# A fused attention and mixture-of-experts layer on one core: coefficient rows by DMA from HBM in place of a selector matmul, and three PSUM banks each for gate and up

## What is computed

```
scores = sigmoid(x @ router_w.T);  topk_idx, topk_w = route(x)      # 8 of 64 experts, from 4 of 8 groups
coef = zeros((T, E)).at[arange(T)[:, None], topk_idx].add(topk_w)
g = einsum('th,ehi->tei', x, Wg);  u = einsum('th,ehi->tei', x, Wu)
h = silu(g) * u * coef[:, :, None]
moe_out = einsum('tei,eih->th', h, Wd)
shared = silu(x @ SWg) * (x @ SWu) @ SWd
x + moe_out + shared
```

## Time and profile before

| what | value |
|---|---|
| median of 3 runs (lowest to highest) | 1395.52 us (1395.37 to 1397.26) |
| time of the profiled execution | 1397.18 us |
| its span, first to last instruction | 1395.5 us |
| PE, busy share of the span | 97% |
| POOL | 81% |
| DVE | 77% |
| ACT | 63% |
| mean granted TensorE clock | 0.990 |

### The profile page before, as it was taken

The page is one execution under the profiler, slowest core; times in us unless marked ns, Lnnn a source line. Parts: engine busy times, 40 slices in busy tenths (PEclk is TensorE's granted clock), DMA queues, the critical chain, the costliest instruction groups (busy, mean ns, idle before and its releaser), DMA issues.

```text
span 1395.5 us, 37217 instructions
## 1 busy us (share of the span) xinstructions
PE 1347.2 (97%) x12985; PEld 776.2 (56%) x12985; DVE 1075.9 (77%) x1906; ACT 875.9 (63%) x1588; POOL 1130.1 (81%) x2235
## 2 busy tenths in 40 slices
PE   3999999999999999999988999999999999999998
PEld 1566666666666666666656544444444444444443
DVE  6788888877888877888878778687777777786765
ACT  4677766666666666666666565656565655656554
POOL 2888888888888888888988887878786877878776
PEclk8899999999999999999999999999999999999999
DMA  7233333333333333333321000000000000000000
GB/s 188 72 81 76 81 76 81 75 83 78 84 75 83 83 83 78 79 77 79 89 58 47 9 1 8 9 9 8 4 15 0 16 1 16 1 16 0 1 8 8
DMA packets 84851, 67.60 MB, mean 48 GB/s; under 512 B 27793, under 2 KB 75217, under 8 KB 84689
## 3 DMA queue, kind: packets, MB, share of 16 engines
q1 hardware_dynamic: 84688, 65.52, 18.9%
HBM read 13.05 MB, written 2.10 MB: 11 GB/s over the span
## 4 chain that ended last, share of the span: by engine, by line
PE 77%; DVE 8%; issue 5%; POOL 5%; ACT 3%; SPq 1%; DMA 1%; DVEq 0%; ACTq 0%; POOLq 0%
PE bank L1048 74%; POOL arena L532 3%; DVE arena L1006 3%; PE bank L1234 2%; POOL arena L494 1%; DVE arena L1012 1%; ACT arena L690 1%; DVE arena L951 1%; DMA arena<-in_L_attn_bk 0%; ACT arena L650 0%; ACT arena L654 0%; DVE arena L901 0%; PE bank L1258 0%; ACT arena L671 0%; DVE arena L971 0%
## 5 line engine op out<-in xcount | busy, mean ns | idle before, releaser
L1048 PE MATMUL bank<-arena 128*128 128x512 f16 (+4 forms) x12600 | 1318.4, 265 | 33.0 <-DVE arena L982 7.3
L1048 PEld LDWEIGHTS bank<-arena 128*128 128x128 f16 (+2 forms) x12600 | 731.9, 98 | 586.2 <-DVE arena L1012 21.0
L494 POOL TENSOR_TENSOR arena<-arena 128x256 f16<-128x256 f32 x1024 | 597.2, 615 | 101.4 <-ACT arena L650 100.5
L532 POOL TENSOR_TENSOR arena<-arena 128x128 f16<-128x128 f32 x1056 | 423.1, 436 | 118.3 <-ACT arena L695 114.6
L951 DVE TENSOR_REDUCE arena<-bank 128x2 f32<-128x1024 f32 x256 | 312.1, 1220 | 53.8 <-PE bank L1048 49.7
L650 ACT ACTIVATE arena<-bank 128x512 f32<-128x512 f32 x512 | 276.8, 595 | 63.2 <-PE bank L1048 63.2
L695 ACT ACTIVATE arena<-arena 128x512 f16<-128x512 f32 x264 | 165.7, 628 | 158.6 <-DVE arena L1012 157.0
L1006 DVE TENSOR_TENSOR arena<-arena,bank 128x512 f32<-128x512 f32 x256 | 175.2, 684 | 108.1 <-ACT arena L690 79.9
L1012 DVE TENSOR_TENSOR arena<-arena,bank 128x512 f32<-128x512 f32 x256 | 176.1, 688 | 29.3 <-DVE arena L1006 4.5
L690 ACT ACTIVATE arena<-bank 128x512 f32<-128x512 f32 x264 | 154.9, 587 | 56.8 <-PE bank L1048 54.0
L639 ACT ACTIVATE arena<-bank,arena 128x512 f16<-128x512 f32 x128 | 88.0, 687 | 143.0 <-PE bank L1048 143.0
(11 more groups left out here) (107 smaller groups left out, 426.3 us busy)
## 6 DMA issues: line engine op xcount, KB each, us to landing
arena<-arena SPq DMA_DIRECT2D x384, 128.0 KB, 2.4
arena<-in_L_attn_x SPq DMA_DIRECT2D x9, 256.0 KB, 2.9
arena<-in_L_ffn_Wg SPq DMA_DIRECT2D x32, 64.0 KB, 2.2
arena<-in_L_ffn_Wu SPq DMA_DIRECT2D x32, 64.0 KB, 2.2
arena<-in_L_ffn_Wd SPq DMA_DIRECT2D x32, 64.0 KB, 2.1
out<-arena SPq DMA_DIRECT2D x8, 256.0 KB, 2.3
arena<-in_L_attn_Wq SPq DMA_DIRECT2D x1, 512.0 KB, 3.9
arena<-in_L_attn_Wk SPq DMA_DIRECT2D x1, 512.0 KB, 5.0
```

The lines of the kernel that those rows point to most:

```text
L494: last = pool.tensor_tensor(num_lo[:, u % 2, s, h, q], num[:, u % 2, s, h, q], num_hi[:, u % 2, s, h, q, 1], ALU.subtract)
L532: last = pool.tensor_tensor(hid_lo[:, r, at], hid[:, r, at], hid_hi[:, r, at], ALU.subtract)
L1048: return nc.tensor.matmul(out_, lhsT, rhs, start=start, stop=stop, skip_group_check=True)
```

## The change

The coefficients no longer go through PE. ACT copies the 64 rows to `coef_rows` in SBUF in float32, SP writes them to a scratch tensor in HBM, waits for that, and then for each tile reads the two experts' rows back, each broadcast to 64 partitions, into one of four slots of `coef_b`. DVE multiplies the up bank by the slot, and then that product by the gate bank, on which ACT has applied silu in place. The two banks that the coefficients had go to gate and up, which now have three each. POOL's subtraction is done in two pieces of 256 columns. Piece 31 of DVE (the low half of the coefficients) and the making of the selectors fall away, and tile 0 has a copy of the whole up bank in place of one of two columns.

```diff
-        ps_gate = [ps8[0], ps8[1]]
-        ps_up = [ps8[2], ps8[6]]
-        ps_coef = [ps8[4], ps8[5]]
+        ps_gate = [ps8[0], ps8[1], ps8[4]]
+        ps_up = [ps8[2], ps8[6], ps8[5]]
...
             def run_block(n, r, last):
+                later = not isinstance(n, int) or n > 0
                 sp.wait_ge(coef_sb, n + 1)
-                if not last:
-                    load_x(n + 1, 1 - r)
-                if not isinstance(n, int) or n > 0:
-                    send(n - 1, 1 - r)
+                sp.dma_start(coef_hbm[r], coef_rows[r]).then_inc(coef_out, 16)
+                if not later:
+                    sp.wait_ge(scores_t, 8 * (PAIRS - 2))
+                sp.wait_ge(coef_out, n * 16 + 16)
+                for k in range(1, TILES):
+
+                    if k > 4:
+                        sp.wait_ge(prod_done, n * TILES + (k - 3))
+                    elif later:
+                        sp.wait_ge(prod_done, n * TILES + (k - 4))
+                    for h in range(2):
+                        sp.dma_start(coef_b[h * EXPERT:(h + 1) * EXPERT, (k - 1) % 4, :],
+                                     coef_hbm[r][2 * k - 2 + h:2 * k - 1 + h, :].broadcast_to([EXPERT, S])
+                                     ).then_inc(coef_in[(k - 1) % 4], 16)
+                    if k == 2 and not last:
+                        load_x(n + 1, 1 - r)
+                    if k == 8 and later:
+                        send(n - 1, 1 - r)
...
-                for q in range(QT):
-                    at = slice(q * P, (q + 1) * P)
+                for q in range(2):
+                    at = slice(q * S // 2, (q + 1) * S // 2)
...
                 act.wait_ge(g_ps, t + 1)
-                wait(act, prod_done, t - 2)
-                nc.scalar.activation(silu_g[:, r % 3, :], ps_gate[r % 2], ACT.Silu).then_inc(silu_done, 1)
+                nc.scalar.activation(ps_gate[r % 3], ps_gate[r % 3], ACT.Silu).then_inc(silu_done, 1)
...
-                dve.wait_ge(silu_done, t + 1)
                 dve.wait_ge(u_ps, t + 1)
                 if k > 0:
-                    nc.vector.tensor_tensor(prod[:, i % 2, :], silu_g[:, i % 3, :], ps_up[i % 2],
+                    j = k - 1
+                    dve.wait_ge(coef_in[j % 4], n * (EP // 4 * 32) + (j // 4 + 1) * 32)
+                    nc.vector.tensor_tensor(prod[:, i % 2, :], coef_b[:, j % 4, :], ps_up[i % 3],
                                             ALU.mult).then_inc(prod_done, 1)
-                    dve.wait_ge(prod_done, t + 1)
+                else:
+
+                    nc.vector.tensor_copy(prod[:, i % 2, :], ps_up[i % 3]).then_inc(prod_done, 1)
+                dve.wait_ge(silu_done, t + 1)
+                dve.wait_ge(prod_done, t + 1)
                 wait(dve, hid_lo_done, t - 5)
...
+                nc.vector.tensor_tensor(hid[:, i % 6, :], prod[:, i % 2, :], ps_gate[i % 3],
+                                        ALU.mult).then_inc(hid_done, 1)
...
-                wait(pe, silu_done, t - 1)
-                product(ps_gate[i % 2], w_hi[:, k, 0, :], w_lo[:, k, 0, :], fT_hi[r], fT_lo[r]).then_inc(g_ps, 1)
-                wait(pe, prod_done, t - 1)
-                product(ps_up[i % 2], w_hi[:, k, 1, :], w_lo[:, k, 1, :], fT_hi[r], fT_lo[r]).then_inc(u_ps, 1)
-                if k > 0:
-                    if k == 1:
-                        pe.wait_ge(coef_lo, n + 1)
-                    wait(pe, hid_done, t - 1)
-                    mm(ps_coef[(k - 1) % 2], spread[:, k - 1, :], coef_split[r], True, True).then_inc(coef_ps, 1)
+                wait(pe, hid_done, t - 2)
+                product(ps_gate[i % 3], w_hi[:, k, 0, :], w_lo[:, k, 0, :], fT_hi[r], fT_lo[r]).then_inc(g_ps, 1)
+                wait(pe, prod_done, t - 2)
+                product(ps_up[i % 3], w_hi[:, k, 1, :], w_lo[:, k, 1, :], fT_hi[r], fT_lo[r]).then_inc(u_ps, 1)
```

More of the change, by code:

```diff
@@ L52 @@
 DVE_0 = {0: (1,), 1: (2,), 2: (3,), 9: (7,), 10: (8,), 15: (12,), 21: (16,), 22: (17,), 23: (18, 19), 24: (20, 21),
-         25: (22, 23), 26: (24,), 27: (25,), 28: (26,), 29: (27,), 30: (28,), 31: (31,)}
+         25: (22, 23), 26: (24,), 27: (25,), 28: (26,), 29: (27,), 30: (28,)}
 POOL_0 = {0: (1,), 2: (2,), 3: (3,), 7: (6,), 10: (8,), 20: (14,)}
@@ L59 @@
 DVE_N = {1: (1,), 2: (2,), 3: (3,), 8: (7,), 9: (8,), 15: (12,), 19: (16,), 20: (17,), 21: (18, 19), 22: (20, 21),
-         23: (22, 23), 24: (24,), 25: (25,), 26: (26,), 27: (27,), 28: (28,), 31: (31,)}
-POOL_N = {2: (2,), 3: (3,), 6: (6,), 9: (8,), 17: (14,)}
+         23: (22, 23), 24: (24,), 25: (25,), 26: (26,), 27: (27,), 28: (28,)}
+POOL_N = {3: (3,), 5: (2,), 6: (6,), 9: (8,), 17: (14,)}
 ACT_N = {5: (4,), 6: (5,), 11: (9,), 12: (10,), 14: (11,), 17: (14,), 30: (30,)}
@@ L151, in layer @@
         tri = take(G * G)
-        twice = take(E)
         assert top[0] <= xT_hi_at + dead
@@ L156, in layer @@
         fT_hi, fT_lo = ([f16(take(S // 2))] for _ in range(2))
-        coef_split = [f16(take(S // 2))]
+        coef_rows = [take(S)[0:E, :]]
         scores = tiles4(take(QT * E))
@@ L164, in layer @@
         top[0] = stack_at
-        spread = f16(take(E * EXPERT // 2)).rearrange("p (t n) -> p t n", t=EP)
+        coef_b = take(4 * S).rearrange("p (r q) -> p r q", r=4)
         xin.append(tiles4(take(S)))
@@ L169, in layer @@
             ring.append(f16(take(S // 2)))
-        coef_split.append(f16(take(S // 2)))
         top[0] = stack_at + 2 * 2 * 4 * S // 2
-        silu_g = take(3 * S).rearrange("p (r q) -> p r q", r=3)
+        coef_rows.append(take(S)[0:E, :])
         prod = take(2 * S).rearrange("p (r q) -> p r q", r=2)
@@ L177, in layer @@
         assert top[0] <= stack_at + 4 * 2 * 4 * S // 2 + 2 * 4 * S // 2
+        coef_hbm = [nc.dram_tensor(f"coef_rows{i}", (E, S), F32, kind="Internal").ap() for i in range(2)]
         bank = [ctx.enter_context(nc.psum_tensor(f"bank{i}", [P, 1024], F32)) for i in range(4)]
@@ L254, in layer @@
         route_step = sem("route_step")
-        coef_lo = sem("coef_lo")
-        spread_done = sem("spread_done")
-        coef_ps = sem("coef_ps")
+        coef_out = sem("coef_out")
+        coef_in = [sem(f"coef_in{i}") for i in range(4)]
         tri_done = sem("tri_done")
@@ L451, in route @@
                                        channel_multiplier=0).then_inc(tri_done, 1)
-                    pool.tensor_tensor(twice, ident[:, 0:E], ident[:, E:P], ALU.add).then_inc(tri_done, 1)
                 if k in (3, 8):
@@ L477, in route @@
                                        beta_b.unsqueeze(1).broadcast_to([P, QT, D]), ALU.add).then_inc(xbeta, 1)
[L479 to L484, removed]
             def run(p, u, batch):
@@ L520, in run @@
                     split_weights()
-                if isinstance(p, int) and p == PAIRS - 2:
-                    selectors()
             steps(run, pool)
@@ L625, in route @@
                     act.wait_ge(coef_t, m + 1)
-                    nc.scalar.activation(coef_split[r][0:E, :], bank_c(m)[0:E, :], ACT.Copy).then_inc(coef_sb, 1)
+                    wait(act, coef_out, (m - 1) * 16)
+                    nc.scalar.activation(coef_rows[r], bank_c(m)[0:E, :], ACT.Copy).then_inc(coef_sb, 1)
             def run(p, u, batch, slots=range(4)):
@@ L929, in route @@
                     own(nc.vector.reciprocal(share, total))
[L930 to L933, removed]
                 if k == 28:
@@ L1253, in down, with transpose_sum @@
                         start=k == 0, stop=k == TILES - 1).then_inc(down_done, 1)
-            def transpose_sum(n):
+            def transpose_sum(n, last):
                 pe.wait_ge(y_copied, n + 1)
+                if not last:
+                    pe.wait_ge(coef_sb, n + 2)
                 for k in range(QT):
@@ L1272, in run_block @@
                             route(n + 1, 1 - r, part)
-                transpose_sum(n)
+                transpose_sum(n, last)
             pe.wait_ge(w_split, TILES - 1)
@@ L1278, in _ @@
                 if k == 1:
-                    pe.wait_ge(coef_lo, 1)
-                    pe.wait_ge(spread_done, 1)
+                    pe.wait_ge(coef_sb, 1)
                 gate_up(0, 0, k)
```

9 lines of the change are left out of this document (removed).

## The result

The changed kernel takes 1361.52 us (median of 4 runs, 1358.09 to 1363.27) against 1395.64 us (the kernel before with a fourth run): a ratio of 0.975, 95% interval 0.9728 to 0.9772, 34 us faster. The profiled execution took 1363.3 us with a span of 1361.5 us.

The account below looks back on a forecast made before the run. PE's matmuls bound the expert part. Seven blocks save 6.9 less 2.5 us each (30.8), the last 6.9 and 0.3, less 2.3 at the start: 35.7 us, so 1397.2 becomes 1361.5, median 1360 us; range 1342 to 1393.

Parts of the forecast that it names:

- What bounds the kernel: Expert part: PE's matmuls are the bound, 0.216 us each; a tile takes 1.94 us in place of 2.16.
- The waits of the kernel before: PE in a block before the change: 72.9 us of work against 74.9 and 77.1 measured, so 2.0 and 4.2 us waits.
- The sum: Whole kernel: seven routed blocks gain 4.4 us each, the last 6.9 and 0.3, less 2.3 at the start: 35.7 us.
- The last block's 6.9: Last block, without routing: its 32 fewer matmuls of 0.216 us save 6.9 us, with nothing given back.
- The 0.3 us for POOL's last step: End of the last block: POOL's last step becomes 0.3 us shorter, counted as gain.
- DVE in the routing stretch: Ten routing tiles per block: DVE lags and PE waits for its second product, net 1.4 us more; bounds 0 and 3.2.
- POOL: Tile 6 of routed blocks: routing piece 6 stands ahead of the low half on POOL's queue, 0.7 us; bounds 0 and 1.5.
- Silu in PSUM, and the steady reads: Every tile: ACT's PSUM write and SP's two row loads, 1.1 us per tile if engines are full, cost nothing.
- The block's start: Tile 1 of a block: coefficients' way through HBM makes DVE 1.2 us late, costing 0.4 us per block; bounds 0 and 3.
- The first block: Start of the expert part: nothing runs ahead, rows land 2.9 us late, costing 2.3 us; bounds 0 and 3.5.
- The rule that speaks against it: Coefficient row reads: at the skill's 103 GB/s a tile takes 2.5 us, over 1.94; slow-reads rival 0.18.

## Why the prediction was right, point by point

- *What bounds the kernel.* Right. In the last stretch a tile takes 9 matmuls at 0.216, and 28 fewer matmuls save 6.1 us.
- *The waits of the kernel before.* Read wrongly. The working took a block's length less 72.9 us for waits, 2.0 and 4.2 us. By the earlier trace rows itself PE was idle for 0.8 and 2.2 us; the rest is time that counts as busy.
- *The sum.* 35.7 us of gain forecast, 34.1 measured between the medians; blocks of 71.6 us by its working (66.0 + 3.1 + 2.5), 71.5 on average over the six. The last block's 6.9 is 6.1 in the table, since PE runs four tiles ahead and four of the 32 matmuls lie in the stretch before. The 0.3 us for POOL's last step did not come: PE waits 0.84 us for it, where it was 0.85. Over the six stretches PE's idle time grew by 2.4 us a block (1.3 to 3.7) against 2.5 put down. Its parts were less exact than their sum, and that is luck: 1.2 for routing against 1.4, 0.4 for POOL against 0.7, 0.8 for the copy of the sum against 0.4. The low clock behind the long waits was in no term.
- *DVE in the routing stretch.* Right in place and kind: PE waits for the second product (L1014) three times there, 2.0 us. Before, PE waited for DVE's first product in the same stretch of block 3, 0.43 and 0.20 us, and 0.23 us for silu shortly ahead of it, so it is 1.2 to 1.4 us more. The difference came as put down, its two terms did not: 3.0 had been worked out for after and 1.6 for before, and 2.0 and 0.6 to 0.9 were measured. The two-bank run shows that the lag of the third banks is real: without them the stretch has 3.2 us. That POOL's longer pieces stretch DVE's operations was not in the sum. It takes 0.24 us for each of the two operations named there (L875, L905).
- *POOL.* At tile 6 PE waits 0.78, 0.86, 0.17 and 0.78 us in four of the six stretches and not at all in two, 0.4 us on average against 0.7: right in place, somewhat small. That two pieces gain there is shown by the run with four.
- *Silu in PSUM, and the steady reads.* Right, they cost nothing. Landing was 2.9 us and not 2.4, an issue 0.58 us as in the attention part, both inside the cover; the DMA share is 0.41 at 125 GB/s over a block, 0.5 at 135 had been forecast.
- *The block's start.* The mechanism was right for the plain starts and the first one, down to the copy of the sum; the size was not. 0.4 us a block had been put down. Without the round trip the seven starts together give 7.2 us (2.3 at the first block's end, 4.9 over the six stretches), 1.0 us each. Part of that is the clock, which fell three times in the changed kernel and once in that run. The 2.1 to 2.2 us where the loop turns, for 0.9 before, are not the round trip's, as that run shows; no term had their growth.
- *The first block.* 2.3 us put down as a delay, 2.8 measured, by what the run without the round trip has won at tile 11: right. DVE's first routed product begins 1.6 us later than before by the clock of the two traces, and 2.8 us later counted from the transposes of the coefficients.
- *The rule that speaks against it.* By the figure of the Trainium skill ("DMA: Bandwidth & Descriptors", Latency and other measured facts) the time would have risen. It did not: over a block the DMAs moved 125 GB/s, and a row of 2 KB read 64 times lands 0.2 us later than 64 rows. The case that the Trainium skill has there, rows of one transfer megabytes apart, was tried in no run here. What made the start's broadcasts slow was neither a limit per address at that size nor a price per packet, and is open: the slow place lies at the very beginning, behind a transfer of 4 KB that the kernel makes in pieces of 4 bytes, and no run took that one away.

Where my expectations failed was in the runs: the dead matmul, POOL in one piece, what was hoped for from the earlier copy and the later piece 3, the turns of the loop in the run without the round trip, and the upper bound for one address.

## What to carry to other kernels

When the bound engine loses work, first work out how far the next one may lag, in buffers, for each part hides or uncovers the other: here all but the fewer matmuls gained 12.5 us, all but the extra banks 12.6, the whole 34. A buffer that a removed step sets free can be worth as much as the step. A round trip through memory is hidden in mid-stream and shows at every place where the stream starts anew: here 7.2 us at seven block starts and 2.8 at the first block. So look for its price there and at the engine that stands in order behind the late one. After a change that lets the matrix engine wait longer in one piece, look at the granted clock behind the wait: here three waits of 2.1 to 2.2 us cost some 5 us more, by the estimate above.

## What was not expected of the hardware

GpSimd's pieces set the length of small operations of VectorE in SBUF that begin while a piece runs: 510, 753 and 1239 ns for the same 128 columns beside pieces of 431, 679 and 1169 ns. Products with one operand in PSUM did not feel it (688 ns throughout). The Trainium skill ("SBUF — State Buffer", SBUF: two separate sides) says that the two engines share a pair of ports as an exclusive lock, held for a whole instruction, by VectorE for operations with two SBUF inputs among others; the three rows agree with it. The Trainium skill also has it that whichever of the two begins first keeps the pair, and the two pairs of rows of the one-piece run agree with that too. The scalar operation on 4 columns (L858, 1.16 us beside a piece of 1.15) has one SBUF input. The same sentence of the Trainium skill also counts operations in a two-port mode; that L858 ran in one, no row shows. A kernel that makes GpSimd's work cheaper by longer pieces pays with VectorE's latency, and of the three lengths tried the best, 256 columns, lies between.
